# Cross attention with heads of width 64: low parts of q and k one step on, a head's normalization spread over more steps, three raw buffers, output products at other steps

## The chip, the cores and the metric

One core of a Trainium2 chip runs the whole program. The metric is the device time in microseconds of one execution. Three runs of the kernel before took 2144.26, 2138.64 and 2145.36 us; the median is 2144.26 us.

## The reference

The program is a decoder of two layers in fp32 on x of shape (4, 512, 256). Each layer adds an attention-like block, a cross attention and a feed-forward block, each followed by a layer norm. The change lies in the cross attention of the second layer:

```python
def _L1_xattn_ref(x, context, Wq, Wk, Wv, Wo, bo):
    B, N, D_MODEL, H, DH = (2, 512, 256, 16, 64)
    SCALE = DH ** (-0.5)
    q = (x @ Wq).reshape(b, n, H, DH)
    k = (context @ Wk * SCALE).reshape(b, m, H, DH)
    v = (context @ Wv).reshape(b, m, H, DH)
    scores = jnp.einsum('bihd,bjhd->bhij', q, k)
    attn = jax.nn.softmax(scores, axis=-1)
    out = jnp.einsum('bhij,bjhd->bihd', attn, v)
    return out.reshape(b, n, H * DH) @ Wo + bo
```

It is called with four batches of 512 rows, so there are 4 x 16 = 64 heads, each with a 512 x 512 softmax. x = layernorm(x + this) follows.

## The kernel before, in words

The function `cross_heads` is this stage. Every operand of the large products is held as a pair of fp32r tiles, a high and a low part; the product of two pairs is three matmuls (high x high, high x low, low x high). For q and k of one head the parts are stacked: `qs` has q's high part in partitions 0 to 63 and its low part in 64 to 127, `ks` has k's high part in both halves, `q2` and `k2` the rest with one more row that carries the row maxima.

The work is one loop over steps `s`, written out by hand for each engine (`pe`, `act`, `dve`, `pool`, `sp`); a step is one tile of 128 rows of one head, so a head has 4 steps (TB), a batch 64 (STEPS) and the stage 256 (END). Each engine runs its own list in order and waits on semaphores. In step s:

- TensorE (`pe`) computes the scores of tile s into one of two MAX_BANKS (L1893), then the transposed scores of tile s - 7 (L1903, L1904) into one of two ST_BANKS, then the weighted sum with V of tile s - 10 (L1917 to L1919) into the OUT_BANK of the head. In every fourth step it transposes the four row maxima of a head (L1928) into ROW_BANK.
- VectorE (`dve`) takes the row maximum of tile s from the MAX_BANK (L2049).
- ScalarE (`act`) takes the exponential of tile s - 7 twice: as the high part `STp_hi` (L1981) and in fp32 as `ST` (L1985).
- GpSimd (`pool`) takes the low part of tile s - 8: `STp_lo` = ST - STp_hi (L2134).

Between these stand, at fixed steps: the q projection of two heads in step 3 of each 8 (bank SPARE) and the k projection in step 5 (ROW_BANK), L1842; ScalarE's high parts of q and k at 3, 5 and twice at 6 (L2028, L2030); VectorE's low parts at the same steps (L2079, L2082), which free the bank; GpSimd's copy of q's high part into `q2` at 3 and 6 (L2140); SyncE's copy of k's high part into the other half of `ks` by DMA (L2179). The row transpose of step 0 writes ROW_BANK and so waits until both low parts of k have been taken. Value projections stand at the steps of VALUES, the input transposes at steps 56 and 57, and the load of the next context (512 KB, L2164) at step 40 of a batch. GpSimd adds the bias to x at steps 46 to 49 (L2146).

A head is normalized after its last weighted sum. ScalarE copies the bank to `raw` (L1993, 13 steps after the head's first tile). The row of sums goes by DMA into a 32 x 16 tile `folded` (L2187, step 15), VectorE takes its reciprocal (L2088, 16), a DMA writes it to memory (L2195, 17), another reads it back broadcast over 64 partitions into `rinv` (L2203, 19), and VectorE multiplies: `attT` = raw x rinv (L2095, 20). All small DMAs of this chain, the row copies (L2170) and the K copies are issued by SyncE in the order of steps.

The output projection is taken in four parts a batch (OUTS): half n of the heads, half z of the rows, 16 matmuls each into SPARE (L1875), added to `summed` by VectorE (L2105). They wait for the attT of heads 7 and 15.

Of the kernel before, what the change touches and what calls it, by code (L numbers as in the profile page):

```python
# [14 lines left out]
TB = S // P  # L15
# [1734 lines left out]
def cross_heads(kit):  # L1750

    nc, T, X, ident, bank = kit.nc, kit.T, kit.X, kit.ident, kit.bank
    PE, A, V, G, SP = nc.tensor, nc.scalar, nc.vector, nc.gpsimd, nc.sync
    summed, stats, mv, veps, rstd, mhalf = kit.summed, kit.stats, kit.mv, kit.veps, kit.rstd, kit.mhalf
# [2 lines left out]
    MAX_ROW, ROWS = HD, HD + 1  # L1760
    STEPS = H1 * TB
    ROW_LAG, ST_LAG, OUT_LAG = 4, 7, 10
    NHI, NFULL, FOLD = 3, 2, 16
    END = B * STEPS
    LOW_SHARE = False
    with ExitStack() as ph:
        def sb(name, shape, dt=f32):
            return kit.sb(name, shape, dt, ph)
# [13 lines left out]
        V_hi, V_lo = sb("V_hi", [P, TB, H1, HD + 1], f32r), sb("V_lo", [P, TB, H1 * HD], f32r)  # L1782
        attT = sb("attT", [P, GROUPS, S])
        stage = attT.rearrange("p g s -> p (g s)").rearrange("p (k c n) -> p k c n", k=2, c=DC)
        raw = [sb("raw%d" % z, [HD + 1, S]) for z in range(2)]
        rinv = [sb("rinv%d" % z, [HD, S]) for z in range(2)]
        folded, inverse = ([sb("%s%d" % (n, z), [S // FOLD, FOLD]) for z in range(2)] for n in ("folded", "inverse"))
        rinv_d = kit.rinv_d
# [40 lines left out]
            return divmod(n, GROUPS) if x == 0 and 0 <= n < B * GROUPS else None  # L1829

        VALUES = ((0, 0, 0, SPARE), (0, 1, 0, ROW_BANK), (2, 2, 0, SPARE), (2, 3, 0, ROW_BANK), (9, 0, 1, SPARE), (10, 1, 1, SPARE), (16, 2, 1, SPARE), (17, 3, 1, SPARE))
        OUTS = ((50, 0, 0), (58, 0, 1), (STEPS + 24, 1, 0), (STEPS + 25, 1, 1))
        FIRST, LAST = -STEPS + 40, END + 46

        def out_u(h, b):
            return b * STEPS + h * TB + TB - 1

        def pe():
            def group(out, pairs):
# [125 lines left out]
        def act():  # L1965
# [8 lines left out]
            for s in range(FIRST, LAST):  # L1974
                u = s - ST_LAG
                if 0 <= u < END:
                    bk = ST_BANKS[u % 2]
                    A.wait_ge(bk.full, bk.full_at["scores", u])
                    if u >= NHI:
                        A.wait_ge(weighed.sem, weighed[u - NHI])  # L1980
                    A.activation(STp[u % NHI][0], bk.ap, ACT.Exp)  # L1981
                    if u >= NFULL:
                        before = low[low_by[u - NFULL]]
                        A.wait_ge(before.sem, before[u - NFULL])
                    A.activation(ST[u % NFULL], bk.ap, ACT.Exp).then_inc(bk.free, 1)  # L1985
                u = s - OUT_LAG
                if 0 <= u < END and u % TB == TB - 1:
                    b, h, _ = place(u)
                    bk = OUT_BANKS[h % 2]
                    A.wait_ge(weighed.sem, weighed[u])  # L1990
                    if b or h > 1:
                        A.wait_ge(att_done.sem, att_done[(b, h - 2) if h > 1 else (b - 1, h - 2 + H1)])
                    A.activation(raw[h % 2], bk.ap[0:HD + 1], ACT.Copy).then_inc(bk.free, 1)  # L1993
                u = s - ROW_LAG
                if 0 <= u < END and u % TB == 0:
                    b, h, _ = place(u)
                    A.wait_ge(ROW_BANK.full, ROW_BANK.full_at["row", b, h])
                    if b or h > 1:
                        A.wait_ge(rowed[h % 2].sem, rowed[h % 2][(b, h - 2) if h > 1 else (b - 1, h - 2 + H1)])
                    A.activation(rowbuf[h % 2], ROW_BANK.ap[0:TB, 0:P], ACT.Copy).then_inc(ROW_BANK.free, 1)  # L2000
                b = of_batch(s, 54 - STEPS)
                if b is not None:
                    A.wait_ge(ctx_in.sem, ctx_in[b])
                    if b:
                        A.wait_ge(ROW_BANK.full, ROW_BANK.full_at["k", b - 1, GROUPS - 1])
                    A.activation(ctxp[0], ctxT, ACT.Copy).then_inc(ctx_high.sem, ctx_high.inc(b))
                for c in range(DC):
                    b = of_batch(s, 56 + c - STEPS)
                    if b is not None:
                        A.wait_ge(SPARE.full, SPARE.full_at["x2", b, c])  # L2010
                        A.activation(srcp[0][:, c, :], SPARE.ap, ACT.Copy).then_inc(src_high.sem, src_high.inc((b, c)))
                for r, t, n, bk in VALUES:
                    b = of_batch(s, r)
                    if b is not None:
                        A.wait_ge(bk.full, bk.full_at["v", b, t, n])
                        if b:
                            A.wait_ge(weighed.sem, weighed[(b - 1) * STEPS + (n + 1) * STEPS // 2 - 1])
                        A.activation(V_hi[:, t, n * 8:(n + 1) * 8, 0:HD], bk.ap.rearrange("p (h f) -> p h f", f=HD), ACT.Copy).then_inc(v_high.sem, v_high.inc((b, t, n)))
                for r, of, half in ((3, "q", 0), (5, "k", 0), (6, "q", 1), (6, "k", 1)):
                    p = of_group(s, r)  # L2020
                    if p is not None:
                        b, h = p[0], 2 * p[1] + half
                        z, bk = h % SLOTS, SPARE if of == "q" else ROW_BANK
                        ps = bk.ap[half * HD:(half + 1) * HD]
                        A.wait_ge(bk.full, bk.full_at[of, b, h // 2])
                        head_free(A, b, h)
                        if of == "q":
                            A.activation(qs[z][0:HD], ps, ACT.Copy).then_inc(q_high.sem, q_high.inc((b, h)))  # L2028
                        else:
                            A.activation(ks[z][0:HD], ps, ACT.Copy).then_inc(k_high.sem, k_high.inc((b, h)))  # L2030
                b = of_batch(s, STEPS + 44)
                if b is not None:
                    store_sums(A, b)
                    if b + 1 < B:
                        store_rows(A, b)

        def dve():
# [4 lines left out]
            for s in range(FIRST, LAST):  # L2042
# [23 lines left out]
                for c in range(DC):  # L2066
                    b = of_batch(s, 56 + c - STEPS)
                    if b is not None:
                        V.wait_ge(src_high.sem, src_high[b, c])
                        V.tensor_tensor(srcp[1][:, c, :], SPARE.ap, plain(srcp[0][:, c, :]), ALU.subtract).then_inc(SPARE.free, 1)  # L2070
                for r, of, half in ((3, "q", 0), (5, "k", 0), (6, "q", 1), (6, "k", 1)):
                    p = of_group(s, r)
                    if p is not None:
                        b, h = p[0], 2 * p[1] + half
# [5 lines left out]
                        else:  # L2080
                            V.wait_ge(k_high.sem, k_high[b, h])
                            V.tensor_tensor(k2[z][0:HD], ps, plain(ks[z][0:HD]), ALU.subtract).then_inc(bk.free, 1)  # L2082
                if (s - 16) % TB == 0 and 0 <= s - 16 < END:
                    b, h, _ = place(s - 16)
                    V.wait_ge(folded_in[h % 2].sem, folded_in[h % 2][b, h])
                    if b or h > 1:
                        V.wait_ge(rinv_out[h % 2].sem, rinv_out[h % 2][(b, h - 2) if h > 1 else (b - 1, h - 2 + H1)])
                    V.reciprocal(inverse[h % 2], folded[h % 2]).then_inc(own.sem, own.inc(("inverse", b, h)))  # L2088
                if (s - 20) % TB == 0 and 0 <= s - 20 < END:
                    b, h, _ = place(s - 20)  # L2090
                    V.wait_ge(rinv_in[h % 2].sem, rinv_in[h % 2][b, h])
                    V.wait_ge(OUT_BANKS[h % 2].free, OUT_BANKS[h % 2].free_at["out", b, h])
                    if b and h % 8 == 0:
                        V.wait_ge(SPARE.full, SPARE.full_at["outs", b - 1, h // 8, 1])
                    V.tensor_tensor(attT[h % 2 * HD:(h % 2 + 1) * HD, h // 2, :], raw[h % 2][0:HD], rinv[h % 2], ALU.mult).then_inc(att_done.sem, att_done.inc((b, h)))  # L2095
                for r, n, z in OUTS:
                    b = of_batch(s, r)
                    if b is not None:
# [23 lines left out]
        def pool():  # L2122
# [4 lines left out]
            for s in range(FIRST, LAST):  # L2127
                u = s - ST_LAG - 1
                if 0 <= u < END and low_by[u] == "pool":
# [2 lines left out]
                    if u >= NHI:  # L2132
                        G.wait_ge(weighed.sem, weighed[u - NHI])
                    G.tensor_tensor(STp[u % NHI][1], ST[u % NFULL], plain(STp[u % NHI][0]), ALU.subtract).then_inc(low["pool"].sem, low["pool"].inc(u))  # L2134
                for r, half in ((3, 0), (6, 1)):
                    p = of_group(s, r)
                    if p is not None:
                        b, h = p[0], 2 * p[1] + half
# [15 lines left out]
        def sp():  # L2154
# [4 lines left out]
            for s in range(FIRST, LAST):  # L2159
# [11 lines left out]
                for r, half in ((5, 0), (6, 1)):  # L2171
                    p = of_group(s, r)
                    if p is not None:
# [3 lines left out]
                        if b or h > 1:  # L2177
                            SP.wait_ge(k_again[z].sem, k_again[z][(b, h - 2) if h > 1 else (b - 1, h - 2 + H1)])
                        SP.dma_start(plain(ks[h % SLOTS][HD:2 * HD]), plain(ks[h % SLOTS][0:HD])).then_inc(k_again[z].sem, k_again[z].inc((b, h)))  # L2179
                u = s - 15  # L2180
                if 0 <= u < END and u % TB == 0:
                    b, h, _ = place(u)
                    z = h % 2
                    SP.wait_ge(OUT_BANKS[z].free, OUT_BANKS[z].free_at["out", b, h])
                    if b or h > 1:
                        SP.wait_ge(own.sem, own["inverse", b if h > 1 else b - 1, h - 2 if h > 1 else h - 2 + H1])
                    SP.dma_start(folded[z], raw[z][HD:HD + 1, :].rearrange("p (a f) -> p a f", f=FOLD)).then_inc(folded_in[z].sem, folded_in[z].inc((b, h)))  # L2187
                u = s - 17
                if 0 <= u < END and u % TB == 0:
                    b, h, _ = place(u)  # L2190
                    z = h % 2
# [1 line left out]
                    if b or h > 1:  # L2193
                        SP.wait_ge(rinv_in[z].sem, rinv_in[z][(b, h - 2) if h > 1 else (b - 1, h - 2 + H1)])
                    SP.dma_start(rinv_d[z].rearrange("(a f) -> a f", f=FOLD), inverse[z]).then_inc(rinv_out[z].sem, rinv_out[z].inc((b, h)))  # L2195
                u = s - 19
                if 0 <= u < END and u % TB == 0:
                    b, h, _ = place(u)
                    z = h % 2
# [487 lines left out]
```

## Time and profile before

| | us |
|---|---|
| median of three runs | 2144.26 |
| the profiled execution | 2145.24 |
| its span, first to last instruction | 2143.9 |
| this stage, first to last score product of the heads | 1173.6 to 1817.8 |

| engine | busy us in the span | share |
|---|---|---|
| TensorE, matmul | 1685.2 | 79% |
| VectorE | 1222.8 | 57% |
| ScalarE | 1035.0 | 48% |
| GpSimd | 976.2 | 46% |

Matmuls overlap each other, so their busy times are longer than the distance at which they start. In the rows below, PE is TensorE, PEld its weight loads, DVE VectorE, ACT ScalarE, POOL GpSimd, SPq the queue of SyncE, and L1893 is line 1893 of the kernel.

### The profile page before, as it was taken

To read this page: it belongs to the slowest core of one execution; us is meant where nothing else is said; L and a number is where in the kernel's file an instruction comes from. 1 tells how busy PE (TensorE), PEld (TensorE's weight loads), DVE (VectorE), ACT (ScalarE), POOL (GpSimd) and SP (SyncE) were. 2 spreads that over 40 slices of the span, in tenths; PEclk is the share of its full clock that TensorE was granted. 3 is DMA by queue.
4 is the path that set the end of the run, shared out by engine and by line. 5 is a ranking of instruction groups with operands and counts; after the bars stand their busy time and mean duration, and the time that the engine had idled before them with its cause. 6 is when DMAs were issued, how large, how long until landed. Compare 5 with 4: busy or idle time off the path is not lost. (4 is left out here: it accounts for less than half of the span.)

```text
span 2143.9 us, 23819 instructions
## 1 busy us (share of the span) xinstructions
PE 1685.2 (79%) x7419; PEld 1232.0 (57%) x7419; DVE 1222.8 (57%) x2325; ACT 1035.0 (48%) x1979; POOL 976.2 (46%) x816
## 2 busy tenths in 40 slices
PE   5488895899935787878882888998988998669892
PEld 3376674687733565656652556665655666456661
DVE  5455554666646685959853555565565565352224
ACT  1143443555511584857772665665755666242220
POOL 0000001343323474756770565665555566138884
PEclk9789998899975798989995999999999999869996
DMA  1130001444335221313002010111111111128776
GB/s 52 49 105 1 30 20 56 148 123 127 70 86 128 70 45 51 73 40 89 21 1 96 21 41 22 30 55 26 26 38 41 31 28 45 63 62 194 184 180 160
DMA packets 96787, 146.17 MB, mean 68 GB/s; under 512 B 22711, under 2 KB 61820, under 8 KB 93830
## 3 DMA queue, kind: packets, MB, share of 16 engines
q1 hardware_dynamic: 64960, 102.68, 16.6%
q0 software_dynamic: 18432, 26.36, 6.8%
q10 hardware_dynamic: 13270, 15.60, 2.4%
q8 instruction: 61, 1.00, 0.2%
q14 instruction: 64, 0.52, 0.1%
HBM read 101.83 MB, written 36.41 MB: 64 GB/s over the span
## 5 line engine op out<-in xcount | busy, mean ns | idle before, releaser
L2134 POOL TENSOR_TENSOR STp_lo_use<-ST_use,STp_hi_use 128x512 fp32r<-128x512 f32 x256 | 336.7, 1327 | 104.9 <-ACT ST_use L1985 101.1
L1667 POOL TENSOR_TENSOR STp_lo<-ST,STp_hi 128x512 fp32r<-128x512 f32 x192 | 254.2, 1341 | 142.7 <-ACT ST L1435 142.0
L1981 ACT ACTIVATE STp_hi_use<-bank 128x512 fp32r<-128x512 f32 x256 | 152.9, 597 | 178.1 <-PE bank L1919 174.9
L1431 ACT ACTIVATE STp_hi<-bank 128x512 fp32r<-128x512 f32 x256 | 158.8, 620 | 83.4 <-PE bank L1369 82.8
L1556 DVE TENSOR_REDUCE nmax<-bank 128x1 f32<-128x512 f32 x256 | 168.9, 680 | 42.2 <-PE bank L1358 41.8
L1358 PE MATMUL bank<-rows_k,rows_q 65*128 65x512 f32 x256 | 126.0, 501 | 62.9 <-DVE nmax L1556 44.3
L2049 DVE TENSOR_REDUCE nmax_use<-bank 128x1 f32<-128x512 f32 x256 | 170.1, 682 | 6.9 <-PE bank L1893 4.2
L1435 ACT ACTIVATE ST<-bank 128x512 f32<-128x512 f32 x256 | 160.1, 625 | 0.0
L1985 ACT ACTIVATE ST_use<-bank 128x512 f32<-128x512 f32 x256 | 151.7, 593 | 2.2 <-POOL STp_lo_use L2134 2.2
L1893 PE MATMUL bank<-ks,qs 128*128 128x512 f32 x256 | 112.2, 440 | 25.2 <-DVE nmax_use L2049 13.2
L2140 POOL CAST q<-qs 64x512 fp32r<-64x512 f32 x64 | 40.0, 625 | 197.7 <-ACT qs L2028 195.5
L870 POOL TENSOR_SCALAR veps<-mv 128x4 f32<-128x4 f32 x4 | 0.9, 228 | 271.8 <-DVE mv L819 271.8
L1369 PE MATMUL bank<-rows_q,rows_k 66*128 66x512 f32 x256 | 112.3, 439 | 3.1 <-ACT ST L1435 2.3
L1358 PEld LDWEIGHTS bank<-rows_k,rows_q 65*128 65x128 f32 x256 | 54.0, 212 | 104.1 <-DVE nmax L1556 71.1
L2564 POOL DMA_INDIRECT acc_scratch<-res,sidx_all x64 | 102.0, 1594 | 24.2 <-issue 17.7
L1381 PE MATMUL bank<-STp_hi,Vone 128*128 128x512 f32 x256 | 108.0, 422 | 0.7 <-POOL STp_lo L1667 0.7
L1382 PE MATMUL bank<-STp_lo,Vone 128*128 128x512 f32 x256 | 107.0, 418 | 0.0
L1917 PE MATMUL bank<-STp_hi_use,V_hi 128*65 128x512 f32 x256 | 102.7, 401 | 1.1 <-POOL STp_lo_use L2134 1.1
L1903 PE MATMUL bank<-qs,ks 128*128 128x512 f32 x256 | 102.0, 398 | 1.1 <-DMA q<-rowbuf_use 1.0
L1904 PE MATMUL bank<-q,k 65*128 65x512 f32 x256 | 102.2, 399 | 0.0
L2079 DVE TENSOR_TENSOR qs<-bank,qs 64x512 fp32r<-64x512 f32 x64 | 44.1, 689 | 101.5 <-ACT qs L2028 101.3
L1919 PE MATMUL bank<-STp_lo_use,V_hi 128*65 128x512 f32 x256 | 101.7, 397 | 0.0
(425 smaller groups left out, 4610.6 us busy)
## 6 DMA issues: line engine op xcount, KB each, us to landing
stage<-in_W SPq DMA_DIRECT2D x16, 1024.0 KB, 4.9
Wgu<-in_Wgu SPq DMA_DIRECT2D x32, 384.0 KB
rows_q<-hop_scratch SPq DMA_DIRECT2D x32, 256.0 KB, 4.3
ks<-ks SPq DMA_DIRECT2D x64, 128.0 KB, 2.3
rinv<-rinv_scratch SPq DMA_DIRECT2D x64, 128.0 KB, 3.0
rows_k<-hop_scratch SPq DMA_DIRECT2D x24, 256.0 KB, 5.5
hop_scratch<-qkp_hi SPq DMA_DIRECT2D x20, 256.0 KB
Wda<-in_Wdn SPq DMA_DIRECT2D x32, 128.0 KB
```

Of the source, the lines that this page charges most:

```text
L1358: PE.matmul(bk.ap, rows_q[0:MAX_ROW, h, j * P:(j + 1) * P], rows_k[0:MAX_ROW, h, :], start=True, stop=True).then_inc(bk.full, 1)
L1369: PE.matmul(bk.ap, rows_k[:, h, kt * P:(kt + 1) * P], rows_q[:, h, :], start=True, stop=True).then_inc(bk.full, 1)
L1381: PE.matmul(bk.ap, Vone[:, kt, h, :], STp[u % NHI][0], start=k == 0 and kt == 0, stop=False)
L1431: A.activation(STp[u % NHI][0], bk.ap, ACT.Exp)
L1435: A.activation(ST[u % NFULL], bk.ap, ACT.Exp).then_inc(bk.free, 1)
L1556: V.tensor_reduce(nmax[:, i % 2, h % HS * TB + j:h % HS * TB + j + 1], bk.ap, AX.X, ALU.max, negate=True).then_inc(bk.free, 1)
L1667: G.tensor_tensor(STp[u % NHI][1], ST[u % NFULL], plain(STp[u % NHI][0]), ALU.subtract).then_inc(low["pool"].sem, low["pool"].inc(u))
L1893: PE.matmul(bk.ap, qs[z][:, j * P:(j + 1) * P], ks[z], start=True, stop=True).then_inc(bk.full, 1)
L1981: A.activation(STp[u % NHI][0], bk.ap, ACT.Exp)
L1985: A.activation(ST[u % NFULL], bk.ap, ACT.Exp).then_inc(bk.free, 1)
L2049: V.tensor_reduce(nmax[:, (h % 2) * TB + j:(h % 2) * TB + j + 1], bk.ap, AX.X, ALU.max, negate=True).then_inc(bk.free, 1)
L2134: G.tensor_tensor(STp[u % NHI][1], ST[u % NFULL], plain(STp[u % NHI][0]), ALU.subtract).then_inc(low["pool"].sem, low["pool"].inc(u))
```

## The change

VectorE's low parts of q and k come one step later (4, 6, 7, 7 in place of 3, 5, 6, 6), and so does GpSimd's copy of q (4 and 7 in place of 3 and 6). `raw` has three buffers in place of two. The reciprocal of a head is taken at step 17 in place of 16, written at 19 in place of 17, read back at 21 in place of 19, and attT is taken at 24 in place of 20. The output products of the first half of the heads stand at steps 58 and 65 in place of 50 and 58.

```diff
-    NHI, NFULL, FOLD = 3, 2, 16
+    NHI, NFULL, NRAW, FOLD = 3, 2, 3, 16
-        raw = [sb("raw%d" % z, [HD + 1, S]) for z in range(2)]
+        raw = [sb("raw%d" % z, [HD + 1, S]) for z in range(NRAW)]
-        OUTS = ((50, 0, 0), (58, 0, 1), (STEPS + 24, 1, 0), (STEPS + 25, 1, 1))
+        OUTS = ((58, 0, 0), (STEPS + 1, 0, 1), (STEPS + 24, 1, 0), (STEPS + 25, 1, 1))
+        RAW_LAG, INVERSE_LAG, RINV_OUT_LAG, RINV_LAG, ATT_LAG = 15, 17, 19, 21, 24
+        def nth(b, h):
+            return b * H1 + h
...
# act
-                    if b or h > 1:
-                        A.wait_ge(att_done.sem, att_done[(b, h - 2) if h > 1 else (b - 1, h - 2 + H1)])
-                    A.activation(raw[h % 2], bk.ap[0:HD + 1], ACT.Copy).then_inc(bk.free, 1)
+                    if nth(b, h) >= NRAW:
+                        A.wait_ge(att_done.sem, att_done[divmod(nth(b, h) - NRAW, H1)])
+                    A.activation(raw[nth(b, h) % NRAW], bk.ap[0:HD + 1], ACT.Copy).then_inc(bk.free, 1)
...
# dve
-                for r, of, half in ((3, "q", 0), (5, "k", 0), (6, "q", 1), (6, "k", 1)):
+                for r, of, half in ((4, "q", 0), (6, "k", 0), (7, "q", 1), (7, "k", 1)):
...
-                if (s - 16) % TB == 0 and 0 <= s - 16 < END:
-                    b, h, _ = place(s - 16)
+                u = s - INVERSE_LAG
+                if 0 <= u < END and u % TB == 0:
+                    b, h, _ = place(u)
...
-                if (s - 20) % TB == 0 and 0 <= s - 20 < END:
-                    b, h, _ = place(s - 20)
+                u = s - ATT_LAG
+                if 0 <= u < END and u % TB == 0:
+                    b, h, _ = place(u)
...
# pool
-                for r, half in ((3, 0), (6, 1)):
+                for r, half in ((4, 0), (7, 1)):
...
# sp
-                u = s - 15
+                u = s - RAW_LAG
...
-                u = s - 17
+                u = s - RINV_OUT_LAG
...
-                u = s - 19
+                u = s - RINV_LAG
```

## Rows read from the trace of the kernel before

**Rows 1.** Windows: us; PE, PEld, DVE, ACT, POOL busy (x); clock; DMA share; GB/s.
```profile
1180.00:1820.00 640.00, 568.68 (x2349) 389.40 (x2349) 373.38 (x588) 400.36 (x784) 376.24 (x332) 0.98 0.13 34
1235.77:1252.51 16.74, 14.89 (x64) 9.77 (x62) 9.86 (x16) 12.13 (x24) 11.60 (x10) 1.00 0.13 34
```

**Rows 2.** Timeline of PE: start us, us, what, idle before and what ended it.
```profile
1226.64 0.47 PE L1893 MATMUL bank<-ks,qs 128*128 128x512 f32 x1 [0.28 <-DMA ks<-ks]
...
1229.10 0.27 PE L1928 MATMUL bank<-ident,nmax_use 128*4 128x128 f32 x1 [0.82 <-DVE nmax_use L2049]
...
1230.60 0.40 PE L1893 MATMUL bank<-ks,qs 128*128 128x512 f32 x1
1230.83 0.40 PE L1903 MATMUL bank<-qs,ks 128*128 128x512 f32 x1
...
1232.86 0.50 PE L1893 MATMUL bank<-ks,qs 128*128 128x512 f32 x1 [0.69 <-DVE nmax_use L2049]
```

**Rows 3.** Waits of 1165 to 1865 us: who waits <- for whom: total, times, longest.
```profile
DVE attT L2095 <- DMA rinv<-rinv_scratch: 38.7, 25, 2.3
...
PE bank L1928 <- DVE nmax_use L2049: 30.5, 31, 2.5
...
PE bank L1893 <- DVE nmax_use L2049: 13.2, 12, 2.5
PE bank L1893 <- DMA ks<-ks: 12.0, 27, 3.1
```

**Rows 4.** Timeline of DVE, the same steps.
```profile
1226.81 0.69 DVE L2079 TENSOR_TENSOR qs<-bank,qs 64x512 fp32r<-64x512 f32 x1 [1.28 <-ACT qs L2028]
1227.53 0.69 DVE L2082 TENSOR_TENSOR k<-bank,ks 64x512 fp32r<-64x512 f32 x1
1228.26 1.29 DVE L2049 TENSOR_REDUCE nmax_use<-bank 128x1 f32<-128x512 f32 x2
...
1231.40 0.68 DVE L2095 TENSOR_TENSOR attT<-raw,rinv 64x512 f32<-64x512 f32 x1 [1.39 <-DMA rinv<-rinv_scratch]
1232.11 1.29 DVE L2049 TENSOR_REDUCE nmax_use<-bank 128x1 f32<-128x512 f32 x2
```

**Rows 5.** Timeline of SyncE's queue, the same steps.
```profile
1228.48 0.59 SPq L2203 DMA_DIRECT2D rinv<-rinv_scratch  x1
```

**Rows 6.** DMA issues of 1165 to 1865 us: count, KB each, median us to landing.
```profile
ks<-ks SPq DMA_DIRECT2D x64, 128.0 KB, 2.3
rinv<-rinv_scratch SPq DMA_DIRECT2D x64, 128.0 KB, 3.0
...
rinv_scratch<-inverse SPq DMA_DIRECT2D x64, 2.0 KB, 1.8
```

**Rows 7.** Timeline at steps 40 to 43 of batch 0.
```profile
1262.62 0.58 SPq L2164 DMA_DIRECT2D ctxT_use<-in_ctxT  x1
...
1263.25 0.66 SPq L2170 DMA_DIRECT2D q<-rowbuf_use  x1
...
1268.10 0.50 PE L1893 MATMUL bank<-ks,qs 128*128 128x512 f32 x1 [2.46 <-DVE nmax_use L2049]
```

**Rows 8.** DMA issues of 1262 to 1267 us.
```profile
rinv_scratch<-inverse SPq DMA_DIRECT2D x1, 2.0 KB, 3.1
```

**Rows 9.** Windows, a stretch of low clock (columns as in rows 1).
```profile
1268.63:1272.04 3.41, 3.41 (x9) 2.32 (x8) 0.70 (x2) 1.44 (x3) 1.27 (x1) 0.50 0.17 44
```

**Rows 10.** Timelines of DVE, POOL and PE at steps 48 to 50 of batch 0.
```profile
1285.06 4.13 DVE L2095 TENSOR_TENSOR attT<-raw,rinv 64x512 f32<-64x512 f32 x1 [1.52 <-DMA rinv<-rinv_scratch]
...
1284.79 0.72 POOL L2146 TENSOR_TENSOR summed<-X,bo_use 128x256 f32<-128x256 f32 x1
...
1289.33 5.27 PE L1875 MATMUL bank<-Wo_use,attT 128*128 128x256 f32 x16 [3.49 <-DVE attT L2095]
```

**Rows 11.** Line L2095: durations in ns, least, median, most.
```profile
L2095 DVE TENSOR_TENSOR attT<-raw,rinv x64: 616/947/4303, 1221.3 to 1840.9; 64x512 f32<-64x512 f32 x64
```

**Rows 12.** Timeline of DVE at step 32 of batch 1.
```profile
1416.48 1.37 DVE L2095 TENSOR_TENSOR attT<-raw,rinv 64x512 f32<-64x512 f32 x1 [1.49 <-DMA rinv<-rinv_scratch]
```

More of the change, by code:

```diff
@@ L1831, in cross_heads @@
         VALUES = ((0, 0, 0, SPARE), (0, 1, 0, ROW_BANK), (2, 2, 0, SPARE), (2, 3, 0, ROW_BANK), (9, 0, 1, SPARE), (10, 1, 1, SPARE), (16, 2, 1, SPARE), (17, 3, 1, SPARE))
-        OUTS = ((50, 0, 0), (58, 0, 1), (STEPS + 24, 1, 0), (STEPS + 25, 1, 1))
+        OUTS = ((58, 0, 0), (STEPS + 1, 0, 1), (STEPS + 24, 1, 0), (STEPS + 25, 1, 1))
+        RAW_LAG, INVERSE_LAG, RINV_OUT_LAG, RINV_LAG, ATT_LAG = 15, 17, 19, 21, 24
         FIRST, LAST = -STEPS + 40, END + 46
-        def out_u(h, b):
-            return b * STEPS + h * TB + TB - 1
+        def nth(b, h):
+            return b * H1 + h
         def pe():
@@ L2094, in dve @@
                         V.wait_ge(SPARE.full, SPARE.full_at["outs", b - 1, h // 8, 1])
-                    V.tensor_tensor(attT[h % 2 * HD:(h % 2 + 1) * HD, h // 2, :], raw[h % 2][0:HD], rinv[h % 2], ALU.mult).then_inc(att_done.sem, att_done.inc((b, h)))
+                    V.tensor_tensor(attT[h % 2 * HD:(h % 2 + 1) * HD, h // 2, :], raw[nth(b, h) % NRAW][0:HD], rinv[h % 2], ALU.mult).then_inc(att_done.sem, att_done.inc((b, h)))
                 for r, n, z in OUTS:
@@ L2186, in sp @@
                         SP.wait_ge(own.sem, own["inverse", b if h > 1 else b - 1, h - 2 if h > 1 else h - 2 + H1])
-                    SP.dma_start(folded[z], raw[z][HD:HD + 1, :].rearrange("p (a f) -> p a f", f=FOLD)).then_inc(folded_in[z].sem, folded_in[z].inc((b, h)))
-                u = s - 17
+                    SP.dma_start(folded[z], raw[nth(b, h) % NRAW][HD:HD + 1, :].rearrange("p (a f) -> p a f", f=FOLD)).then_inc(folded_in[z].sem, folded_in[z].inc((b, h)))
+                u = s - RINV_OUT_LAG
                 if 0 <= u < END and u % TB == 0:
```

## The prediction

> **What bounds the kernel now.** I read the stage's busy times first: of 640 us in its middle TensorE is busy 568.68 at a granted clock of 0.98, VectorE 373, ScalarE 400, GpSimd 376 [rows 1]. That looks TensorE-bound, but a matmul's 0.40 us overlap the next one: they start 0.23 us apart (1230.60, 1230.83) [rows 2]. A step of the loop therefore needs 6 x 0.23 = 1.38 us of TensorE, and a projection (six more) another 1.38. Eight steps hold two projections and two row transposes of 0.1: 14.0 us. An undisturbed stretch of eight takes 16.74 [rows 1], so 2.7 us of it is waiting, in three places.
>
> I count steps modulo 8, and step 0 starts at 1226.64. Its row transpose comes at 1229.10, where 1226.64 + 1.38 = 1228.02 was possible: it waits for step 7's maximum. Step 2 lasts 1232.86 - 1230.60 = 2.26 us against 1.38: the next score product needs the bank that step 1's maximum frees. And step 0 itself began 0.4 us late, for the DMA that copies K into the lower half [rows 2]. The list of waits has the first place 31 times, 30.5 us; the second as L1893 <- nmax; the third 27 times, 12.0 us [rows 3].
>
> Why the maxima are late stands on VectorE's timeline [rows 4]. In step 6 it takes the low parts of the second q and k head in one go, for which ScalarE's high parts aren't ready (1.28 us idle); q's runs 1226.81 to 1227.50, k's 1227.53 to 1228.22, and step 7's maximum, whose scores TensorE had begun at 1224.8, only follows at 1228.26. In step 0 the same queue stands 1.39 us before attT, for the DMA of the reciprocals, so the maxima of steps 1 and 2 run from 1232.11. Over the stage attT <- rinv is 38.7 us [rows 3].
>
> **The change part by part.** The sums are made in the profiled execution: its own time is 2145.24 us, its span 2143.9; the median of the runs is 2144.26, so no correction is worth making.
>
> *Low parts one step later.* No instruction is added. VectorE now takes step 7's maximum before the two low parts. The high parts are where they were, so k's low part still ends at 1228.22, and the transpose then waits for that (it frees the bank) instead of for 1228.95: 0.73 us earlier. The wait that is left, about 0.35 us, is ScalarE's. This holds in 28 of the 31 cases; in the three of step 56 the low part of the next context (1.2 us) stands ahead and I count nothing. **A: 28 x 0.73 = 20.4 us**, between 0 and the 30.5 of the whole wait [rows 3]. GpSimd's copy of q moves too, behind one more low part of STp; it then ends about 3.3 us after step 7 begins and is needed five steps on, so it costs nothing. SyncE's K copy isn't moved: the 0.4 us before step 0 stays.
>
> *Normalization spread out.* The folded row is loaded at the same step, the reciprocal is taken one step later (17), written two later (19), broadcast two later (21), multiplied four later (24). Before, the broadcast was issued at 1228.48, behind a K copy for which SyncE had waited, and takes 3.0 us to land [rows 5, 6]; VectorE was ready for it at 1230.0. Now it is issued three steps ahead of its use, right behind the first K copy (or the row copy): there before it is needed. attT then runs straight behind step 0's maximum. Counting from step 7's start: maximum 3.4 to 4.1, attT from 4.14; GpSimd is in a low part until 4.9; attT 4.9 to 5.45; step 1's maximum to 6.15. TensorE wants its bank after steps 7, 0, 1 and 2, at 1.82 + 1.77 + 1.48 + 1.38 = 6.45 (step 7 with the 0.4 for K, step 0 with the 0.3 that A leaves). The wait in step 2 goes, by 0.3 us. It is listed 12 times with 13.2 us [rows 3], and each is 0.19 longer (0.69 shown at 1232.86 where 2.26 - 1.38 = 0.88 are lost): 15.5 us. The longest are the two where the broadcast was late and attT met a low part (2.46 at 1268.10 [rows 7]). 1.1 us stays, where a value projection sits in the step. Behind 1268.10 and its twin in batch 2, once TensorE had stood idle, the granted clock fell to 0.50 (1.2 GHz) for 3.41 us [rows 9], which costs half of that: 2 x 1.7 = 3.4 us more. Against it: the row copy of step 41 stands behind the 512 KB context load of step 40, and TensorE now gets there sooner; it is issued 0.6 us after the load [rows 7]. A 2 KB copy behind that load landed after 3.1 us [rows 8], alone after 1.8 [rows 6], and TensorE wants the row about 1.9 us after its issue: 1.2 us of new wait in three batches, -3.6. Three times 0.8 us in step 38, where a late attT met the normalized rows, also goes. **B: 15.5 - 1.1 + 3.4 - 3.6 + 2.4 = 16.6 us**; its ends are 0, if another wait takes each place, and 21.3, if nothing is left.
>
> *Three raw buffers.* raw waits for the attT of three heads before instead of two, but attT is four steps later: the distance is the same one step. It costs nothing where attT is on time; where attT is late ScalarE still stops behind it.
>
> *Output products.* Those of the first half move from steps 50 and 58 to 58 and 65. One is 16 matmuls at 0.215 = 3.4 us at full clock, the work is the same. What matters is step 50. Before, it lasted 10.2 us in three batches and 8.5 in the last, 39.2 together: attT took 4.13 us, TensorE waited 3.49, and its products took 5.27 [rows 10], the first half of them at clock 0.50. GpSimd had a chain of operations without a gap, low parts and sums with the bias (one of them in the rows) in turn, and attT got in after its last one only. The sums stay at steps 46 to 49, and attT still stands in step 48 (of one head earlier). By the distances above it asks at 4.1 us from step 47, and GpSimd's chain of q's copy (0.6), three sums (0.72) and three low parts (1.26) runs from 2.7 to 9.2: attT is done at 9.7, the maximum of step 49 at 10.3, and TensorE starts step 51 at 10.45 instead of 6.45: 4.0 us of wait, and after an idle TensorE that long I take one more stretch at half clock, 1.7 us. Step 50 is 1.38 + 4.0 + 1.7 = 7.1: saved 39.2 - 28.3 = 10.9. The same output products come back at step 65, 3.43 us in three batches (at 65 the bank is free at 4.8 us and TensorE there at 6.0: no wait), and in the last batch into the tail, where TensorE waits for GpSimd anyway: I take 2.0 of at most 3.4. **C: 10.9 - 10.3 - 2.0 = -1.4 us.**
>
> The one price with ends far apart is attT against GpSimd. It is 0.62 us at the least, 0.95 in the median, and 4.3 at the most [rows 11]. Where GpSimd goes from one low part to the next it waits for the running one only (1.37 us at 1416.48 with two low parts side by side [rows 12]): that value I take for step 0. With the sums in between it lost every time (4 of 4): that value I take for step 48.
> The Trainium skill (SBUF — State Buffer, "Who interferes with whom") says that a VectorE instruction with two SBUF inputs and a GpSimd one that reads SBUF hold a shared pair by turns, and that the second one to issue is blocked until the first finishes. The row of 1416.48 agrees; the 4.13 us, across four GpSimd operations, don't. By that rule, attT in step 48 would be done at 5.8 us and step 50 would take some 2.1: rival 1.
>
> **Sum: 20.4 + 16.6 - 1.4 = 35.6; 2145.24 - 35.6 = 2109.6, I say 2110 us.**
>
> **Rivals.**
> 1. *attT gets in at step 48 after one operation.* For it: all meetings with low parts alone. Against: the four with the sums. Step 50 is then 1.38 plus 0.75 for GpSimd's backlog: saved 39.2 - 8.5 = 30.7 instead of 10.9. 2109.6 - 19.8 = 2090 us. Chance 0.25.
> 2. *The copies land later.* The broadcast (128 KB) now follows the first K copy within 0.6 us and the row copy likewise; if it takes their share of the DMA engines, step 0 (which already waits 0.4 for K) or step 3 moves; I bound that by 0.7 us, the broadcast's 3.0 less the K copy's 2.3 [rows 6]. 31 x 0.7 = 21.7: 2131 us. Against it: the DMA engines are busy 0.13 [rows 1] and the queue takes them in turn. Chance 0.12.
> 3. *Slower: attT loses the lock in step 0 as well.* GpSimd now has q's copy, then three low parts without a gap from 2.7 to 7.9 us after step 7 begins, and attT asks in the middle. If a chain keeps it out, it ends at 8.45, the maximum at 9.15, and TensorE starts step 3 at 9.25 instead of 6.45: 2.8 us, beside 1.7 of half clock, in the eleven stretches that no long product covers: 49.5 us. 2109.6 + 49.5 = 2159, slower than before. It decides once attT lies past some 3.3 us more than forecast per stretch. Against: attT against low parts was never longer than 1.8 us. Chance 0.08.
> 4. *It changes nothing:* a wait of ScalarE's own paces the steps. Against: its busy time is 400 of 640 us [rows 1], some 12.5 in the 15.2 that eight steps would take. Within 0.3% of 2144. Chance 0.05.
>
> The forecast keeps 0.50. **Chances:** 0.3% is 6.4 us, about what a measurement of this kernel can tell from no change. Faster: 0.50 + 0.25 + 0.12 = 0.87; same 0.05; slower 0.08. The 8-in-10 range reaches from below rival 1 (2084) to above rival 2 (2136).
>
> **What would show it.** Right: PE L1928 <- nmax nearly gone, with a smaller wait for k's low part in its place; attT <- rinv and inverse <- folded near zero; eight plain steps at 15.2 us; step 50 without output products but with an attT of some 5 us beside the sums. Wrong: attT of 0.6 to 1.8 us there (rival 1), L1893 <- ks or L1903 <- q above 20 us (rival 2), attT over 3 us in step 0 (rival 3). The forecast fails altogether if plain stretches stay above 16 us.

## The result

The changed kernel takes 2128.13 us, median of 14 runs (2121.75 to 2138.66), against 2143.65 for the kernel before in as many: ratio 0.9927, 95% interval 0.9908 to 0.9946. It is 15.5 us faster, where 34 had been forecast.

The profiled executions have spans of 2143.9 and 2133.2 us, 10.7 apart. I cut both at the same places: the first and the last score product of the 256 steps (`bank<-ks,qs`, line L1895 now), and the end of the last output product. The forecast's column is the sum of its terms. Both loops begin at 1173.6 us. Loop and tail together are 17.9 us shorter; the last row is a matter of the clock and differs between executions of one kernel too (see below), and so the two profiles are closer than the medians.

| stretch, us | before | after | difference | forecast |
|---|---|---|---|---|
| first to last score product | 644.1 | 621.3 | -22.8 | -37.6 |
| to the end of the last output product | 34.0 | 38.9 | +4.9 | +2.0 |
| the rest (router and experts) | 292.1 | 299.4 | +7.2 | 0 |

Below, the length of a step is the distance from its score product to the next. Windows of the kernel after, its eight plain steps first (24 to 31), then steps 40 to 47, 48 to 55 and 64 to 71 of batch 0, and all that follows the last output product; columns as in [rows 1].

```profile
1225.31:1240.32 15.01, 14.71 (x62) 9.78 (x63) 10.19 (x16) 11.92 (x25) 11.74 (x11) 1.00 0.14 37
1255.36:1273.86 18.50, 16.45 (x63) 10.75 (x63) 10.20 (x16) 11.87 (x25) 12.39 (x12) 0.91 0.21 57
...
1273.86:1297.14 23.28, 16.49 (x62) 10.74 (x63) 15.18 (x17) 14.69 (x29) 15.51 (x15) 0.91 0.10 27
...
1320.29:1344.16 23.87, 23.57 (x103) 17.35 (x103) 12.87 (x21) 14.44 (x29) 11.36 (x11) 1.00 0.09 24
1833.85:2133.20 299.35, 219.91 (x947) 162.93 (x948) 110.27 (x299) 66.94 (x166) 177.60 (x138) 0.83 0.62 149
```

The same windows of the kernel before, the plain one aside (16.74, [rows 1]).

```profile
1260.12:1280.11 19.99, 16.44 (x62) 10.74 (x63) 10.91 (x16) 12.11 (x25) 11.57 (x10) 0.91 0.21 54
1280.11:1304.77 24.66, 20.07 (x79) 13.86 (x79) 13.90 (x17) 12.16 (x25) 14.26 (x14) 0.93 0.09 22
...
1328.81:1350.04 21.23, 20.13 (x87) 14.34 (x87) 12.44 (x20) 14.44 (x29) 11.63 (x10) 1.00 0.10 26
1851.78:2143.90 292.12, 212.12 (x949) 155.00 (x948) 110.22 (x299) 66.85 (x166) 177.52 (x138) 0.86 0.63 153
```

The plain stretch is as forecast (15.2). The next two hold as many matmuls (62 or 63), and take 3.5 and 8.3 us more. The waits of 1165 to 1865 us after the change, to be read against [rows 3].

```profile
PEld bank L1895 <- DVE nmax_use L2051: 15.9, 4, 4.2
PE bank L1895 <- DVE nmax_use L2051: 14.0, 4, 3.7
...
PEld bank L1930 <- DVE k L2084: 12.9, 26, 0.7
...
PE bank L1895 <- DMA ks<-ks: 11.9, 26, 3.1
PEld bank L1905 <- DMA q<-rowbuf_use: 11.8, 13, 3.2
DVE attT L2099 <- DMA rinv<-rinv_scratch: 11.1, 5, 3.0
```

attT <- rinv fell from 38.7 to 11.1. The transpose (L1930) no longer waits for a maximum but for k's low part, 26 times up to 0.7 us. The maxima hold TensorE back four times only, once a batch. The wait of L1905, the matmul behind the score product, for the row copy has grown: 11.8 us in 13 places, where it was 3.2 us in 5. The 11.1 us that are left of attT <- rinv lie with the last five heads, behind about 1797 us.

**Where the chain broke.** VectorE (first fence), SyncE's queue (second) and TensorE (third) of the kernel after, at steps 40 to 43 of batch 0.

```profile
1256.22 0.69 DVE L2084 TENSOR_TENSOR k<-bank,ks 64x512 fp32r<-64x512 f32 x1
1256.95 0.69 DVE L2051 TENSOR_REDUCE nmax_use<-bank 128x1 f32<-128x512 f32 x1
1257.56 1.42 DVE L2099 TENSOR_TENSOR attT<-raw,rinv 64x512 f32<-64x512 f32 x1
```

```profile
1257.78 0.41 SPq L2168 DMA_DIRECT2D ctxT_use<-in_ctxT  x1
1258.32 0.66 SPq L2174 DMA_DIRECT2D q<-rowbuf_use  x1
```

```profile
1259.87 0.39 PE L1895 MATMUL bank<-ks,qs 128*128 128x512 f32 x1
1262.06 0.72 PE L1905 MATMUL bank<-qs,ks 128*128 128x512 f32 x1 [1.81 <-DMA q<-rowbuf_use]
1262.57 0.63 PE L1906 MATMUL bank<-q,k 65*128 65x512 f32 x1
```

attT in step 0 is on time and takes 1.42 us, as forecast. The row copy, 2 KB behind 512 KB on one queue, is in use 3.7 us after its issue (1258.32, 1262.06), and TensorE has stood idle for 1.81 us by then. In batch 1 it is 4.2 us, with 2.72 idle. Then its matmuls take 0.63 us instead of 0.40: the granted clock is at the lower level, 1.2 GHz.

```profile
1262.17:1265.58 3.41, 3.41 (x9) 2.33 (x10) 0.00 (x0) 1.00 (x2) 0.43 (x1) 0.50 0.02 5
```

Eight steps later attT (VectorE) meets GpSimd's chain, second fence.

```profile
1276.12 5.53 DVE L2099 TENSOR_TENSOR attT<-raw,rinv 64x512 f32<-64x512 f32 x1
1281.58 0.67 DVE L2051 TENSOR_REDUCE nmax_use<-bank 128x1 f32<-128x512 f32 x1
```

```profile
1275.97 1.29 POOL L2138 TENSOR_TENSOR STp_lo_use<-ST_use,STp_hi_use 128x512 fp32r<-128x512 f32 x1
1277.23 0.74 POOL L2150 TENSOR_TENSOR summed<-X,bo_use 128x256 f32<-128x256 f32 x1
1277.93 1.27 POOL L2138 TENSOR_TENSOR STp_lo_use<-ST_use,STp_hi_use 128x512 fp32r<-128x512 f32 x1
1279.17 0.71 POOL L2150 TENSOR_TENSOR summed<-X,bo_use 128x256 f32<-128x256 f32 x1
1279.85 1.25 POOL L2138 TENSOR_TENSOR STp_lo_use<-ST_use,STp_hi_use 128x512 fp32r<-128x512 f32 x1
```

attT ends 0.55 us after the last of the five (1281.65, 1281.10). TensorE stands idle for 3.71 us, and 3.41 us behind that are at 0.50. That was in the forecast. This was not: VectorE at steps 54 to 56.

```profile
1294.89 1.45 DVE L2067 TENSOR_TENSOR ctxp_lo_use<-ctxT_use,ctxp_hi_use 128x1024 fp32r<-128x1024 f32 x1 [2.58 <-ACT ctxp_hi_use L2008]
1296.27 0.67 DVE L2084 TENSOR_TENSOR k<-bank,ks 64x512 fp32r<-64x512 f32 x1
```

And TensorE there: step 56's first score product.

```profile
1293.72 0.39 PE L1921 MATMUL bank<-STp_lo_use,V_hi 128*65 128x512 f32 x1
1297.14 0.76 PE L1895 MATMUL bank<-ks,qs 128*128 128x512 f32 x1 [3.03 <-issue]
```

k's first low part, now in step 54, stands behind the context's, which waits 2.58 us for ScalarE. The first score product of a head waits until that part of its k has been taken, so TensorE can't begin step 56, and the score product goes 0.2 us after its end (1296.94, 1297.14). The trace calls the 3.03 us "issue", so the cause is read from VectorE's rows, and tested by a1 below. Step 55 is 4.57 us in batches 0 to 2, where it was 1.8, and 1.82 in batch 3, which loads no next context.

### The profile page after: what moved, and what is told of

Its sections match the earlier page's. It is cut to its first block and busy times, and to the rows that moved or that the text cites. A ratio compares the mean times of both kernels' runs of the same rounds, so it can differ in the third digit from the quotient of the medians.

```text
span 2133.2 us, 23817 instructions
## 1 busy us (share of the span) xinstructions
PE 1702.0 (80%) x7418; PEld 1248.6 (59%) x7419; DVE 1230.0 (58%) x2325; ACT 1030.8 (48%) x1979; POOL 975.2 (46%) x816
## 5 line engine op out<-in xcount | busy, mean ns | idle before, releaser
L1895 PE MATMUL bank<-ks,qs 128*128 128x512 f32 x256 | 113.0, 443 | 35.8 <-DVE nmax_use L2051 14.0
L1905 PE MATMUL bank<-qs,ks 128*128 128x512 f32 x256 | 104.8, 410 | 7.3 <-DMA q<-rowbuf_use 7.2
L1920 PE MATMUL bank<-STp_hi_use,V_lo 128*64 128x512 f32 x256 | 103.4, 404 | 0.0
L2550 POOL DMA_INDIRECT rows<-tokens_scratch,gidx_all x64 | 66.4, 1037 | 71.3 <-DVE sidx_all L2442 52.4
```

The costliest lines, as they stand in the source:

```text
L1895: PE.matmul(bk.ap, qs[z][:, j * P:(j + 1) * P], ks[z], start=True, stop=True).then_inc(bk.full, 1)
```

## The experiments

All ratios are to the kernel before, whose median was 2144.68 us beside the first four, 2145.01 beside the second four and 2143.45 beside the last two. The length of a step is from each kernel's trace.

**a0, the changed kernel again**, for a second profile.

> The changed kernel once more, for a second profile. Its first profile ended 10.7 us earlier than the kernel before, though the heads' score products ended 22.8 us earlier: the tail of the stage gave back 4.9 us, and the router behind it 7.2 us, in 27 us at a granted clock of 0.50. Theory 'the clock behind the stage differs from run to run': this profile's router is not 7 us longer, or another is, and the median stays near 2128. Rival 'the earlier end always meets the low clock': the router again takes 7 us more than before in every profile.

Measured: 2126.43 us (2114.13 to 2137.49), ratio 0.990 (0.987 to 0.993). Score products 621.4 us apart, tail 38.8, rest 299.4: as in the first profile of this kernel. Taken alone this fits the rival, that the earlier end always meets the low clock; the profiles of c1 and c3 below rule it out.

**a1, k's first low part back at step 5.**

```
-  for r, of, half in ((4, "q", 0), (6, "k", 0), (7, "q", 1), (7, "k", 1)):
+  for r, of, half in ((4, "q", 0), (5, "k", 0), (7, "q", 1), (7, "k", 1)):
```

> The changed kernel with the low part of the first k head back at step 5 of 8 (6 in the change). Theory: step 55 grew from 1.8 to 4.6 us in three batches because at step 54 that low part now stands behind the context's low part on VectorE, and the first score product of step 56 waits for its bank: it goes back to 1.8, so 3 x 2.8 = 8 us less, 2120. In the plain stretches VectorE takes the maximum of step 6 after it again, which TensorE has time for: nothing lost. Rival: step 55 waits for the K copy by DMA or for the context's parts themselves, and stays at 4.6: 2128.

Measured: 2117.5 us (2114.3 to 2124.02), ratio 0.9877 (0.985 to 0.9904). Step 55 is 1.80 to 1.86 us in all batches, so the 2.8 us are the queueing on VectorE. A part goes back to step 56 (3.6 to 4.5 us), whose transpose now waits for the second k low part behind the same context. The score products are 12.3 us closer, but 3.4 of that the edit did not aim at: step 43 is 4.41 and 5.00 us in batches 0 and 2, for idle times of 1.36 and 1.94 us with no half clock behind them.

**a2, the context load two steps later**, behind the row copy.

```
-  b = of_batch(s, 40 - STEPS)
+  b = of_batch(s, 42 - STEPS)
```

> The changed kernel with the 512 KB context load issued at step 42 of a batch in place of 40, so behind the row copy of step 41 on SyncE. Theory: step 43 takes 6.4 to 7.3 us in three batches (2.9 without a load) since the row copy lands behind the load, and the idle TensorE then runs at half clock: 43 goes to 2.9, together 3 x 3.8 = 11 us less, 2117. Rival: what stops step 43 is the broadcast of the reciprocals or the copies' own time, and the wait only moves to the row copy of step 45, needed at 47: under 3 us gained.

Measured: 2111.18 us (2108.99 to 2116.59), ratio 0.9844 (0.9816 to 0.9872). Steps 40 to 47 with the load (first fence: batch 0), and SyncE's queue (second).

```profile
1250.03:1264.96 14.93, 14.67 (x63) 9.78 (x63) 10.22 (x16) 11.89 (x25) 12.41 (x12) 1.00 0.24 73
```

```profile
1253.01 0.65 SPq L2174 DMA_DIRECT2D q<-rowbuf_use  x1
...
1254.29 0.58 SPq L2168 DMA_DIRECT2D ctxT_use<-in_ctxT  x1
```

14.93 against 18.50, at full clock. Step 43 is 2.80 to 2.85 us in all four batches, where it was 6.41, 7.26 and 6.43. The load's place in the queue is the whole of that, the stretch of half clock included: 11.6 of the 18.2 us by which the score products come closer. In batch 3 attT at step 48 took 2.37 us instead of 5.5, for which see below; that is 5.8 us more (steps 50 to 52), at which the edit did not aim.

**a3, GpSimd's sums with the bias earlier**, out of the steps that attT meets.

```
-  b = of_batch(s, 46 + t)
+  b = of_batch(s, (42, 43, 45, 46)[t])
```

> The changed kernel with GpSimd's four sums of x and bias at steps 42, 43, 45, 46 in place of 46 to 49. Theory: VectorE's attT at step 48 takes 5.5 us since GpSimd's chain of low parts and sums keeps it out; without sums in the chain it takes 1.4 us, as in the other stretches, steps 50 and 51 fall from 9.7 to 4.3 us and no low clock follows: 4 x 5.4 = 21 us less, 2107. Rival 'the lock is lost to any chain that q's copy starts': attT stays over 4 us. Rival 'it moves': the attT of step 44 takes 4 us or more instead.

Measured: 2097.46 us (2094.47 to 2106.41), ratio 0.9781 (0.9754 to 0.9808). VectorE (first fence) and GpSimd (second) at step 48.

```profile
1276.06 1.42 DVE L2099 TENSOR_TENSOR attT<-raw,rinv 64x512 f32<-64x512 f32 x1
1277.41 0.67 DVE L2051 TENSOR_REDUCE nmax_use<-bank 128x1 f32<-128x512 f32 x1
```

```profile
1275.64 6.88 POOL L2138 TENSOR_TENSOR STp_lo_use<-ST_use,STp_hi_use 128x512 fp32r<-128x512 f32 x5 [0.39 <-ACT ST_use L1987]
```

attT asks 4.05 us after step 47 begins, as in the kernel after; GpSimd is in a low part both times, and five low parts follow each other here. It takes 1.42 us instead of 5.53. Steps 50 and 51 together are 4.2 to 4.6 us instead of 9.7, in four batches: 21.3 us of the 27.9 by which the score products come closer. So moving the sums lets attT in. That a sum is what keeps it out is not shown: with the sums gone GpSimd's low parts also lie differently, and attT asks 0.42 us after one has begun where it had been 0.15. In b1 it asked 0.7 to 1.0 us into a low part, with the sums, and still took 2.7 to 3.0 us; and in b2 it was kept out for 2.2 to 2.3 us ten times with no sum near.

**b1, the low parts alone**: the kernel before with q's and k's low parts and GpSimd's copy of q a step later, the normalization untouched.

> The kernel before with the low parts of q and k and GpSimd's copy of q one step later, and nothing else. Theory: the wait of the row transpose in step 0 of 8 shrinks by 0.8 us in 28 places (22 us), k's low part behind the context's at step 54 costs 3 x 2.8 = 8 us, the 4 us attT at step 48 stays: some 14 us faster, 2130. Rival: with the reciprocals still late, attT takes up what the maxima gained, and it is within 3 us of before.

Measured: 2154.03 us (2148.46 to 2163.47), ratio 1.0055 (1.0036 to 1.0075): slower, a miss of 24 us. In its profile the loop is 1.1 us shorter and the tail 1.1 us longer than before; 6.7 us more lie behind the last output product, with the longer stretch of low clock that is described further down. So the edit alone leaves the loop as long as it was. The plain stretch grew from 16.74 to 17.64. VectorE, SyncE's queue and TensorE of this kernel in it (line numbers of the kernel before).

```profile
1227.57 0.24 DVE L2088 RECIPROCAL inverse<-folded 32x16 f32<-32x16 f32 x1 [0.83 <-DMA folded<-raw]
1229.20 1.62 DVE L2095 TENSOR_TENSOR attT<-raw,rinv 64x512 f32<-64x512 f32 x1 [1.39 <-DMA rinv<-rinv_scratch]
```

```profile
1226.27 0.59 SPq L2203 DMA_DIRECT2D rinv<-rinv_scratch  x1
```

```profile
1227.59 0.40 PE L1893 MATMUL bank<-ks,qs 128*128 128x512 f32 x1
1231.60 0.50 PE L1893 MATMUL bank<-ks,qs 128*128 128x512 f32 x1 [2.44 <-DVE nmax_use L2049]
```

Step 0 is 0.8 us shorter, as in the forecast's A. But attT starts when the broadcast has landed, 2.9 us behind its issue and 4.75 us behind step 0's start (1224.45), as before (4.76, from [rows 2, 4]): it has not come nearer by the 0.8. And it now meets one of GpSimd's low parts (1.62 us instead of 0.68, [rows 4]), 0.94 more. Step 2 is 4.01 us where it was 2.26, longer by 1.75, which is these two. The gain of A is given back in the same eight steps, and with it 0.9 us. Behind the 2.44 us of idle TensorE the clock stays at full speed here.

**b2, the normalization alone**: the kernel after with the low parts and the copy of q where they were.

> The changed kernel with the low parts and the copy of q back at their steps, so the spread normalization, three raw buffers and the moved output products alone. Theory: the wait in step 2 of 8 goes (12 places, 15 us), the row copies behind the context load give back some 11, the output products' move some 2: within 5 us of before, 2140, and the sum of this and the low parts alone is the change's 16 to 17 us. Rival: the two parts need each other, and each alone brings under a quarter of the change.

Measured: 2136.47 us (2121.79 to 2142.96), ratio 0.9947 (0.9921 to 0.9974). Plain stretch 16.23 us; step 0 stays at 2.43, step 2 falls to 1.78. In the profiles this shortens the loop by 15.3 us, b1 by 1.1 and the whole change by 22.8: with the normalization moved the low parts are worth 7.5 us net, alone 1.1. The expected 11 us that the row copies would give back did not show: step 43 is 3.0 to 3.3 us here. A rule of the prediction fails in this run, that where GpSimd goes from one low part to the next attT waits for the running one only (VectorE, first fence; GpSimd, second).

```profile
1226.22 2.27 DVE L2099 TENSOR_TENSOR attT<-raw,rinv 64x512 f32<-64x512 f32 x1
```

```profile
1224.16 3.77 POOL L2138 TENSOR_TENSOR STp_lo_use<-ST_use,STp_hi_use 128x512 fp32r<-128x512 f32 x3
```

attT asks in the second of three low parts and ends 0.56 us after the third (1228.49, 1227.93); ten of the 64 do so.

**c1, the three edits of a1, a2 and a3 together.**

> The changed kernel with the three mends together: k's low part at step 5, the context load at 42, the sums at 42, 43, 45, 46. Theory: they are worth 8, 11 and 22 us at the steps where they act and don't touch each other: 2126 - 41 = 2085, less some 7 us where the router behind the stage no longer meets 27 us of low clock: 2078 to 2085. Rival: the gains overlap, since each also removed low-clock stretches: over 2095.

Measured: 2085.6 us (2080.82 to 2097.11), ratio 0.9742 (0.9711 to 0.9773). The expectation had been 2078 to 2085 us. Steps 40 to 47 and 48 to 55 of batch 0.

```profile
1249.28:1264.21 14.93, 14.69 (x62) 9.77 (x63) 10.79 (x16) 11.88 (x25) 14.54 (x15) 1.00 0.24 71
1264.21:1279.14 14.93, 14.64 (x62) 9.76 (x63) 9.49 (x15) 11.93 (x25) 12.03 (x11) 1.00 0.15 37
```

Both are as long as a plain stretch now. Score products are 583.2 us apart instead of 621.3.

**c2, c1 with the last batch's moved output product at step 60** instead of in the tail.

> The same three mends, and in the last batch the second output product of the first half at step 60 in place of 65 (step 257 of the loop, in the tail). Theory: the change lost 4.9 us between the last score product and the last output product, as that product stands there in front of the weighted sums; now 3.3 of them move into the steps and the tail is as before: 1 to 2 us less than without it. Rival: the tail is longer for another reason, the reciprocals two steps later, and the move costs 3 us more.

Measured: 2089.08 us (2082.07 to 2096.04), ratio 0.9755 (0.9723 to 0.9787): no gain. The tail falls from 37.6 to 34.5 us, near the 34.0 of before, so the moved product is what had made it longer; step 60 of the last batch is 3.3 us longer for it.

**c1 again, and c3 beside it**: c1 with VectorE's low part of the context at step 57.

> The kernel with k's first low part at step 5, the context load at step 42 and GpSimd's sums at steps 42, 43, 45, 46, unchanged, on the same chip as the next. It ran 2085.6 us before; I expect 2081 to 2091, step 56 of the first three batches at 4.5 to 5.0 us.

> The same, with VectorE's low part of the next batch's context at step 57 instead of 54. In the version before it, the row transpose of step 56 waited 2.50 us for k's low part (1283.26), which stood behind the context's (1279.69, 1.46 us) and the maximum and q's low part after it. Theory (the context's low part is the whole of that wait): the wait falls to the 0.4 us of every other stretch, step 56 from 4.97 / 4.65 / 4.49 to about 2.5, and nothing else moves, since VectorE is idle for 2.11 us at step 57: 3 x 2.1 = 6 us less, 2079 us. Rival A: the low part of 1.46 us there delays the source's second low part, for which the output product of step 58 waits (1.09 us): 0 to 3 us less. Rival B: the instruction reads two operands from SBUF and meets GpSimd's low parts at step 57, waits for them and delays the maximum of step 57: no gain.

```
   # VectorE's part; ScalarE's high part stays at 54
-  b = of_batch(s, 54 - STEPS)
+  b = of_batch(s, 57 - STEPS)
```

Measured: c1 again 2094.66 us (2077.27 to 2102.86), ratio 0.9765 (0.9724 to 0.9806); c3 2088.15 us (2080.43 to 2088.86), ratio 0.9741 (0.9711 to 0.977). c1 again had been expected at 2081 to 2091 us and c3 at 2079. The intervals overlap, so the times don't tell the two apart; the traces do, for the loop. Step 56 is 3.09, 3.02 and 3.04 us instead of 4.99, 4.92 and 4.50; its transpose waits 1.02 us instead of 2.50. The score products are 577.8 us apart, against 585.0 and 583.2 in the two profiles of c1 (c1 again first), which is the shortest loop of all. That it is the fastest program isn't shown: its median is above the first one of c1.

## Why the prediction was half right

**Direction and the plain steps: right.** Eight plain steps took 15.01 us, forecast 15.2. Step 0 fell by 0.85 us (0.73 forecast), step 2 to 1.40 us, attT in step 0 took 1.42 (1.37 assumed). The rule behind that last number is too simple, as b2 shows: attT can also wait for one low part more.

**A, 20.4 us: its size held, one sentence failed.** "In the three of step 56 the low part of the next context stands ahead and I count nothing": there the move costs 2.8 us a batch, 8.3 us, on the step ahead of it. I had followed the second q and k low parts past VectorE's queue, not the first k, which the same edit moved behind the context's low part. a1 shows it. About a third of it came back in step 56 itself (4.5 to 3.6 us), 3.0 in all.

**B: the mechanism right, the row copy mis-sized.** 3.6 us for three batches was 1.2 us of wait each. Measured: step 43 at 6.41, 7.26 and 6.43 us against the 4.0 forecast, 8.1 us in all. The waits were 1.81, 2.72 and 1.81 us, since the copy took 3.7 to 4.2 us from issue to use, not 3.1 [rows 8], and the half clock behind each came to 1.7 more. For step 50 I had counted that half clock, here not. a2 shows both go with the load's place.

**C: right.** attT at step 48 took 5.53 us (5.5 forecast); steps 50 and 51 together 9.73 (10.05). The product at step 65 cost 3.3 us of step and 2.6 of its stretch. The tail was mis-sized: +4.9 us for the 2.0 assumed, and c2 shows that the moved product is 3.0 us of the tail.

**After the loop, 7.2 us that no term had.** They come and go without an edit. Windows behind the last output product, and of the stretch at low clock a few us later: c1 (first fence) and c1 again, the same kernel (second).

```profile
1787.94:2079.50 291.56, 212.22 (x949) 155.01 (x948) 110.45 (x299) 66.85 (x166) 177.61 (x138) 0.86 0.63 153
1791.91:1798.74 6.83, 4.46 (x22) 4.49 (x22) 2.66 (x6) 1.19 (x2) 0.00 (x0) 0.50 0.66 202
```

```profile
1794.37:2093.40 299.03, 219.65 (x949) 162.33 (x948) 110.24 (x299) 66.95 (x166) 177.58 (x138) 0.83 0.62 149
1798.78:1826.09 27.31, 23.23 (x106) 21.60 (x107) 12.48 (x66) 3.02 (x5) 0.00 (x0) 0.50 0.33 104
```

TensorE is at the lower level for 6.83 us in one and 27.31 in the other, and the rest of the program is 7.5 us longer. Of twelve profiles, the four in which that stretch begins 3.8 to 4.1 us after the last output product have the short one, the eight in which it begins at 4.3 to 5.2 us the long one. The profile of before has the short one, that of after the long one. The time at which the loop ends doesn't settle it: with the last output product at 1787.94 c1 has the short one, with it at 1788.03 c3 the long one. Of c1's twelve runs the five with a mean granted clock of 0.901 or 0.902 took 2094.6 to 2102.9 us, the seven at 0.905 to 0.907 2077.3 to 2088.0. Part of the runs' spread (17 us in 14 runs of the kernel after) may be this. Another part lies ahead of the loop: in the two profiles of c1 it begins at 1167.2 and 1170.9 us, in the two of the kernel after at 1173.6 and 1176.5. What sets the moment is open, and so is whether the change makes the long stretch more frequent.

**Rivals.** Rival 1 (attT gets in at step 48) didn't happen in the changed kernel, in four of four batches; its price, 20 us, was right: a3 gained 21.3 there by other means. Rival 2: `ks<-ks` stayed at 11.9 us (12.0, [rows 3]); the copy that was late was the row's, for the load, not for the broadcast. Rival 3: no such attT in step 0 of the changed kernel, where it took 1.42 us. Something of its mechanism showed in b2, ten times 2.2 to 2.3 us. Rival 4: no, the plain stretch fell from 16.74 to 15.01 us.

The books of the loop: 37.6 forecast, less 8.1 (step 43) and 8.3 (step 55), plus 3.0 (step 56), gives 24.2; measured 22.8. For the whole, 2.9 us of tail and the 7.2 us behind it lead from there to the 10.7 of the profiles; the medians are 15.5 apart.

## What to carry to other kernels

When an instruction is moved one step, write out what every moved instance lands behind on its engine's queue, in the rare steps too (next batch's loads and splits): here two such places, in three batches each, took 16 us of the 38 forecast for the loop. Small copies that the next product waits for belong ahead of a large load on the same queue, and a wait of TensorE of some 2 us or more should be priced with a stretch of half clock behind it as a likely term, not a sure one. Making one engine's work earlier pays only if the chain that comes next on its queue moves too: the low parts alone left the loop as long as it was. And before a few microseconds are put down to an edit, look where in the program they lie: here up to 3.7 us ahead of the loop and 7.5 us behind it came and went between executions of one kernel.

## What the runs showed of the hardware

- VectorE's multiply of two SBUF operands (attT, 64x512) took 1.42 us when it asked during GpSimd's low parts in an unbroken row of five, and 5.53 us when 128x256 sums stood between them, at the same moment of the step. That isn't fixed either: in batch 3 of a2, with the sums, it took 2.37 us (VectorE, first fence; GpSimd, second).

```profile
1745.15 2.37 DVE L2099 TENSOR_TENSOR attT<-raw,rinv 64x512 f32<-64x512 f32 x1
```

```profile
1745.00 1.28 POOL L2138 TENSOR_TENSOR STp_lo_use<-ST_use,STp_hi_use 128x512 fp32r<-128x512 f32 x1
1746.25 0.73 POOL L2150 TENSOR_TENSOR summed<-X,bo_use 128x256 f32<-128x256 f32 x1
1746.94 1.74 POOL L2138 TENSOR_TENSOR STp_lo_use<-ST_use,STp_hi_use 128x512 fp32r<-128x512 f32 x1
```

  It got in between a sum and a low part, which took 0.46 us longer. Over all profiles attT at this step took 2.4 to 6.2 us in the 28 cases with the sums there, 1.42 or 1.43 in the 20 without. But sums aren't needed for it: ten times in b2 attT stood behind two low parts, 2.2 to 2.3 us. The Trainium skill (SBUF — State Buffer, "Who interferes with whom") has the second to issue blocked until the first finishes; 1.42 and 1.74 us agree; 5.53 and 2.37, during which GpSimd began further operations while VectorE waited, don't. Who wins at a boundary of two GpSimd instructions is open.
- After a wait of TensorE of 1.81 and of 3.71 us the granted clock fell to 0.50 for 3.41 us, which costs 1.7 us each. At the 3.03 us of step 56 it fell too, and the matmuls took 0.63 us. That isn't sure to happen: behind 1.94 us (a1, step 43 of batch 2), 2.44 us (b1, step 26 of batch 0) and 3.49 us (before, step 50 of batch 3) it stayed at full speed. In the twelve profiles, behind the first eight steps of the loop, 52 of the 66 waits of 1.8 to 3.6 us had such a fall by 3.5 us after their end.
- Behind the loop two executions of the same kernel (c1) differ by 7.5 us, with a low stretch of 27.31 or 6.83 us.
